# A graph layer and a ternary feed-forward block: weights transposed by DMA into a ring, and tiles in contiguous rows per group

## The reference

```python
# N=1250 nodes, E=20000 edges sorted by dst, D=512, FFN_DIM=1408, GROUP=128
msg_sum = segment_sum(x[src], dst);  deg = segment_sum(1, dst)
h = x @ W_self + (msg_sum / max(deg, 1)) @ W_neigh + b        # x here: layernorm(x)
h = where(h >= 0, h, 0.01 * h)
x = x + h / max(sqrt(sum(h * h)), 1e-12)

wg = w.reshape(o, i // 128, 128)                               # for w_gate, w_up, w_down
scale = mean(abs(wg)) + 1e-5
wq = clip(round(wg / scale), -1, 1) * scale                    # ternary times a scale
gate = xn @ wq_gate.T;  up = xn @ wq_up.T                      # xn = layernorm(x)
x = x + (silu(gate) * up) @ wq_down.T
```

## Time and profile before

| | before |
|---|---|
| time, median of 3 runs | 364.9 us (363.96 to 366.82) |
| the profiled execution: its own time | 365.24 us |
| the profiled execution: span | 363.3 us |
| mean granted TensorE clock | 0.987 |
| busy: TensorE, weight loads | 329.8 us (91%), 249.6 us (69%) |
| busy: VectorE, ScalarE, GpSimd | 304.6 us (84%), 238.0 us (66%), 163.1 us (45%) |
| chain that ended last, by engine | PE 58%, DVE 26%, ACT 10%, issue 3% |
| the same, line 1320 (the FFN matmuls) | 39% |
| line 1320, matmuls with x as moving operand | 528, 192.4 us busy |
| line 1320, matmuls with h as moving operand | 264, 94.8 us busy |
| line 1114, VectorE's takes of g, u and acc | 260, 167.9 us busy |

### The profile page before, as it was taken

One profiled execution on the slowest core, in us unless ns is written; L12 is line 12 of the kernel. 1 busy time (PEld: TensorE's weight loads), 2 busy tenths in 40 slices (PEclk: granted clock), 3 DMA queues, 4 the chain that ended last, 5 costly groups with the idle time before them and its releaser, 6 DMA issues.

```text
span 363.3 us, 5834 instructions
## 1 busy us (share of the span) xinstructions
PE 329.8 (91%) x1623; PEld 249.6 (69%) x1623; DVE 304.6 (84%) x789; ACT 238.0 (66%) x637; POOL 163.1 (45%) x223
## 2 busy tenths in 40 slices
PE   1997879899999999999687999999999999999992
PEld 0443335554545578777476898989899898889991
DVE  3569999899889248999696998999999989999994
ACT  2155958899787136774656768668777678676670
POOL 7000000110010590110003466888788787799992
PEclk9999999999999999999988999999999999999998
DMA  7961322233232001200000000000000000000215
GB/s 226 291 159 33 86 58 78 68 88 87 59 82 79 3 3 35 74 22 2 0 1 2 0 3 0 3 0 0 2 3 2 0 0 3 0 3 0 73 44 169
DMA packets 9412, 16.69 MB, mean 46 GB/s; under 512 B 1062, under 2 KB 1886, under 8 KB 9378
## 3 DMA queue, kind: packets, MB, share of 16 engines
q1 hardware_dynamic: 9300, 16.21, 15.9%
q10 hardware_dynamic: 78, 0.08, 0.1%
HBM read 13.73 MB, written 2.56 MB: 45 GB/s over the span
## 4 chain that ended last, share of the span: by engine, by line
PE 58%; DVE 26%; ACT 10%; issue 3%; POOL 1%; DVEq 0%; ACTq 0%; POOLq 0%
PE bank L1320 39%; PE bank L1208 7%; PE bank L1250 5%; DVE tq_gu L901 4%; DVE hot_dst L1005 3%; ACT mag_early L690 3%; DVE tq_d L901 2%; DVE hot_src L996 2%; ACT a_t L742 2%; DVE bn L1061 2%; ACT hot_src L675 2%; DVE x_sb L1058 2%; DVE z L1040 1%; PE bank L1232 1%; PE bank L1156 1%
## 5 line engine op out<-in xcount | busy, mean ns | idle before, releaser
L1320 PE MATMUL bank<-x_hi,t_gu 128*128 128x378 f32 (+1 forms) x264 | 96.9, 367 | 3.6 <-DVE x_lo L1075 2.8
L1320 PE MATMUL bank<-x_lo,t_gu 128*128 128x378 f32 (+1 forms) x264 | 95.5, 362 | 0.0
L1208 PE MATMUL bank<-w_sb,xnT 128*125 128x512 f32 x160 | 86.9, 632 | 4.8 <-ACT z L725 4.1
L1114 DVE SCALAR_TENSOR_TENSOR g_acc<-bank,nscale,g_acc 128x378 f32<-128x378 f32 (+1 forms) x99 | 64.3, 650 | 12.1 <-PE bank L1320 10.8
L612 POOL TENSOR_SCALAR thr<-absum 128x4 f32<-128x4 f32 (+1 forms) x34 | 10.7, 315 | 121.5 <-ACT mag_early L690 97.2
L1114 DVE SCALAR_TENSOR_TENSOR u_acc<-bank,nscale,u_acc 128x378 f32<-128x378 f32 (+1 forms) x99 | 64.1, 647 | 0.0
L633 POOL TENSOR_TENSOR acc<-acc,d_one 128x378 f32<-128x378 f32 (+1 forms) x58 | 60.9, 1052 | 0.1
L643 POOL TENSOR_TENSOR hh<-sg,u_acc 128x378 f32<-128x378 f32 (+1 forms) x32 | 35.1, 1098 | 57.4 <-ACT sg L830 57.3
L1320 PEld LDWEIGHTS bank<-x_hi,t_gu 128*128 128x128 f32 x264 | 51.1, 193 | 8.1 <-DVE x_lo L1075 3.5
L1320 PEld LDWEIGHTS bank<-x_lo,t_gu 128*128 128x128 f32 x264 | 51.0, 193 | 3.6
L1167 PEld LDWEIGHTS bank<-hot_dst,hot_src 128*125 128x125 bf16 x157 | 20.8, 137 | 42.0 <-DVE hot_dst L1005 23.0
(11 more groups left out here) (136 smaller groups left out, 558.5 us busy)
## 6 DMA issues: line engine op xcount, KB each, us to landing
raw<-in_L_ffn_w_gate SPq DMA_DIRECT2D x11, 256.0 KB, 2.7
raw<-in_L_ffn_w_up SPq DMA_DIRECT2D x11, 256.0 KB, 2.6
out_x<-x_sb SPq DMA_DIRECT2D x10, 224.0 KB
raw<-in_L_ffn_w_down SPq DMA_DIRECT2D x8, 256.0 KB, 2.7
x_sb<-in_x SPq DMA_DIRECT2D x1, 1344.0 KB
w_sb<-in_L_gnn_W_neigh SPq DMA_DIRECT2D x1, 1024.0 KB, 6.0
w_sb<-in_L_gnn_W_self SPq DMA_DIRECT2D x1, 1024.0 KB, 7.3
raw<-in_L_ffn_w_down SPq DMA_DIRECT2D x4, 192.0 KB, 2.3
```

What stands on the lines that cost most here:

```text
L1114: nc.vector.scalar_tensor_tensor(out=to, in0=bank_of(u, what)[:, 0:w], scalar=nscale[:, j:j + 1], in1=to, op0=ALU.mult, op1=ALU.add).then_ ...
L1208: last = nc.tensor.matmul(to[0:TP, :], xnT[:, t, k * TP:(k + 1) * TP], w_sb[:, k, half * D:(half + 1) * D], start=k == 0, stop=k == KD - 1)
L1320: last = nc.tensor.matmul(to, w, parts[h], start=h == 0, stop=h == 1)
```

## The change

**The weights.** SyncE, behind its last load and a wait for all ternary weights (`sp.wait_ge(ternary, JOBS)`), issues a DMA transpose for each 128x128 block: 8 per gate-and-up turn, 4 per down turn, 22 turns, 132 in all. They go into `turned_gu` (3 slots) and `turned_d` (2 slots), which lie where `raw` was. A turn waits until the Sign copy has emptied its slot. ScalarE's Sign copies stand where they stood, wait for the DMAs of their slot and read the ring. TensorE's 132 weight transposes, the identity `ident_b` and the use of bank 7 for weights are gone; `TERNARY` lists in which turn ScalarE takes which weights. Of `BANK7` only tiles 7, 8 and 9 are left (`XBANK7`).

**The layout.** A group of nodes was tiles of 126 columns each with gaps between them; now its tiles stand side by side with 125 columns, and one more at the end where the sum is odd: widths 376, 376 and 500 (`CN`). `x1_hi` and `x1_lo` are one tensor per group, in which the columns of a k are one run; `acc` follows. The copies of line 762 and 1075 write four rows of 125 or 126 with a stride. `x1_high` waits for all ternary weights from tile 6 on, not from tile 8 on.

```diff
+    CN = [(b - a) * TP + (b - a) % 2 for a, b in CT]
+    C0 = [sum(CN[:c]) for c in range(len(CT))]
...
+    TURN_GU, TURN_D = 3, 2
+    turned_gu = place("turned_gu", [P, TURN_GU, 2 * D], BF16, "raw")
+    turned_d = place("turned_d", [P, TURN_D, D], BF16, "raw", TURN_GU * 2 * D * 2)
...
-    x1_hi = place("x1_hi", [P, NT, KD, TQ], F32R, "w")
-    x1_lo = place("x1_lo", [P, NT, KD * P], F32R, "xz")
+    x1_hi = [place(f"x1_hi{c}", [P, KD, CN[c]], F32R, "w", C0[c] * KD * 4) for c in range(len(CT))]
+    x1_lo = [place(f"x1_lo{c}", [P, KD, CN[c]], F32R, "xz", C0[c] * KD * 4) for c in range(len(CT))]
...
+            sp.wait_ge(ternary, JOBS)
+            for f, down in turns:
+                if (f, down) in old_turn:
+                    sp.wait_ge(t_done, turn_T[old_turn[f, down]] + 1)
+                i = turn_slot[f, down]
+                if not down:
+                    for a in range(2):
+                        for k in range(KD):
+                            sp.dma_start(turned_gu[:, i, a * D + k * P:a * D + (k + 1) * P],
+                                         tq_gu[:, a * NF + f, k * P:(k + 1) * P], transpose=True).then_inc(gu_turned[i], 16)
+                else:
+                    for o in range(KD):
+                        sp.dma_start(turned_d[:, i, o * P:(o + 1) * P], tq_d[:, o, f * P:(f + 1) * P],
+                                     transpose=True).then_inc(d_turned[i], 16)
...
             def ternary_out(f, down):
 
-                act.wait_ge(t_ready, turn_T["T", f, down] + 1)
+                i, uses = turn_slot[f, down], turn_use[f, down] + 1
...
-                    nc.scalar.activation(t_gu[:, t_slot[f], :, :].rearrange("p a d -> p (a d)"), bf(7)[:, 0:2 * D],
+                    act.wait_ge(gu_turned[i], 16 * 2 * KD * uses)
+                    nc.scalar.activation(t_gu[:, t_slot[f], :, :].rearrange("p a d -> p (a d)"), turned_gu[:, i, :],
                                          ACT.Sign).then_inc(t_done, 1)
...
-                    to = bank_of(u, what)[:, 0:width(u)].rearrange("p (t s) -> p t s", s=TQ)
-                    parts = (x1_hi[:, a:b, k, :], x1_lo[:, a:b, k * TQ:(k + 1) * TQ])
+                    parts = (x1_hi[c][:, k, :], x1_lo[c][:, k, :])
...
-                if (u, what) in BANK7:
-                    through_bank7(BANK7[u, what])
+                if (u, what) in XBANK7:
+                    t = XBANK7[u, what]
+                    if t - 1 in XBANK7.values():
+                        pe.wait_ge(xlo_done, t)
+                    transpose_xn(t, normed1, bank[7], x1n_T, place_of(t)[2])
```

More of the change, by code:

```diff
@@ L72, in gnn_ffn, with place_of @@
     TQ = 126
+    GAP = 128
     CT = [(0, 3), (3, 6), (6, NT)]
+    CN = [(b - a) * TP + (b - a) % 2 for a, b in CT]
+    C0 = [sum(CN[:c]) for c in range(len(CT))]
+    NQ = sum(CN)
+    def place_of(t):
+        c = max(c for c in range(len(CT)) if CT[c][0] <= t)
+        a, b = CT[c]
+        rows = TP + (CN[c] - (b - a) * TP if t == b - 1 else 0)
+        return c, (t - a) * TP, rows
     CW = 512
@@ L398, in gnn_ffn @@
             took[p] = 1 + sum(by_act(*q) == by_act(*p) for q in pieces[:i])
-        BANK7 = {(0, "U3"): ("X", 7), (1, "U1"): ("T", 1, 0), (1, "U3"): ("X", 8), (2, "U1"): ("T", 0, 1), (2, "U3"): ("X", 9),
-                 (3, "U3"): ("T", 1, 1), (4, "U3"): ("T", 2, 0), (6, "U3"): ("T", 3, 0), (7, "U3"): ("T", 2, 1),
-                 (8, "U3"): ("T", 3, 1)}
+        TERNARY = {1: (1, 0), 2: (0, 1), 3: (1, 1), 4: (2, 0), 6: (3, 0), 7: (2, 1), 8: (3, 1)}
         for f in range(3, NF - 3):
-            BANK7[first_of[f], "U3"] = ("T", f + 1, 0)
+            TERNARY[first_of[f]] = (f + 1, 0)
             if f < NF - 4:
[L407 to L410, removed]
+                TERNARY[last_of[f]] = (f + 1, 1)
+        for v, what in ((NU - 11, (NF - 1, 0)), (NU - 10, (NF - 2, 0)), (NU - 9, (NF - 3, 1)),
+                        (NU - 8, (NF - 1, 1)), (NU - 7, (NF - 2, 1))):
+            TERNARY[v] = what
         t_slot = [f % 2 for f in range(NF - 1)] + [2]
-        through7 = [("T", 0, 0)] + [BANK7[e] for e in sorted(BANK7)]
-        turn_T = {e: i for i, e in enumerate(e for e in through7 if e[0] == "T")}
+        turns = [(0, 0)] + [TERNARY[v] for v in sorted(TERNARY)]
+        turn_T = {e: i for i, e in enumerate(turns)}
+        assert sorted(turns) == [(f, down) for f in range(NF) for down in range(2)]
+        turn_slot, turn_use = {}, {}
+        for down, slots in ((0, TURN_GU), (1, TURN_D)):
+            for i, e in enumerate(e for e in turns if e[1] == down):
+                turn_slot[e], turn_use[e] = i % slots, i // slots
+        old_turn = {e: old for e in turns for old in turns
+                    if old[1] == e[1] and turn_slot[old] == turn_slot[e] and turn_use[old] == turn_use[e] - 1}
+        XBANK7 = {(0, "U3"): 7, (1, "U3"): 8, (2, "U3"): 9}
+        gu_turned = [sem(f"gu_turned{i}") for i in range(TURN_GU)]
+        d_turned = [sem(f"d_turned{i}") for i in range(TURN_D)]
         piece_ready = sem("piece_ready")
@@ L1224, in _ @@
                     degree_columns(c).then_inc(deg_ready, 1)
-            def ternary_in(f, down):
-                pe.wait_ge(ternary, JOBS if down else JOBS1)
-                if not down:
-                    for a in range(2):
-                        for k in range(KD):
-                            last = nc.tensor.transpose(bf(7)[:, a * D + k * P:a * D + (k + 1) * P],
-                                                       tq_gu[:, a * NF + f, k * P:(k + 1) * P], ident_b[:])
-                else:
-                    for o in range(KD):
-                        last = nc.tensor.transpose(bf(7)[:, o * P:(o + 1) * P], tq_d[:, o, f * P:(f + 1) * P], ident_b[:])
-                last.then_inc(t_ready, 1)
             general_pe(pe, any_outside)
@@ L1294, in _ @@
                             pe.wait_ge(d_added, added[v, f"D{o}"])
+                    c, o, _ = place_of(u)
                     for k in range(KD):
-                        last = nc.tensor.transpose(bank_of(u, what)[0:TP, k * P:(k + 1) * P], acc[:, k, u * TQ:u * TQ + TP], ident[:])
+                        last = nc.tensor.transpose(bank_of(u, what)[0:TP, k * P:(k + 1) * P], acc[:, k, C0[c] + o:C0[c] + o + TP], ident[:])
                     last.then_inc(piece_ready, 1)
```

88 lines of the change are left out of this document (36 added, 52 removed).

## The result

| | before | after |
|---|---|---|
| time, median | 364.95 us (4 runs) | 380.75 us (4 runs, 379.63 to 382.42) |
| ratio | | 1.043, 95% interval 1.038 to 1.048 |
| span of the profiled execution | 363.3 us | 378.3 us |
| mean granted TensorE clock | 0.987 | 0.95 |
| busy: TensorE, VectorE, ScalarE, GpSimd | 329.8, 304.6, 238.0, 163.1 us | 330.5, 303.2, 237.7, 164.5 us |

The changed kernel is 4.3% slower. TensorE has 132 instructions less and is busy as long as before, since it ran for a part of the time at a lower clock (0.95 in the mean); and it waits more.

What follows compares the result with a forecast made beforehand. TensorE bounds the kernel before, SyncE's DMA transposes after: 166.3 + 170.3 + 2.3 = 338.9 us, then 40.2 less 0.7 plus 0.5 gives span 378.9; plus 1.9, about 381 us. Range 351 to 394 us.

Steps and rivals of the forecast that it cites:

- What bounds the kernel, and what takes its place: TensorE bounds at 14.70 us per block; then SyncE's DMA transposes set the pace from about 230 us, 15.6 us per block.
- The pace c: Time from one DMA transpose to the next in SyncE's queue, taken as 1.3 us; break-even at 1.18 us.
- the upper bound: Highest c considered: each DMA transpose lands before the next is issued, 2.3 us, the shortest landing.
- the lower bound: Lowest c considered: what a plain load of 128 rows takes in SyncE's queue, 0.328 us.
- the overlap: Rival: DMA transposes in SyncE's queue overlap, c up to 1.10 us, so weights arrive in time; 354 us, chance 0.38.
- The sum: Whole kernel: last four transposes land at 338.9 us, span 378.9 us, plus 1.9 us gives 380.8, say 381 us.
- The price on TensorE: Weight transposes on TensorE cost 0.305 us plus 0.525 us, so each block gives back 0.83 us.
- The layout: Matmuls on TensorE: x falls to h's step, 0.24 us, and narrower columns save 0.08 us; 0.32 us per block.
- The case on the other side: Rival that DMA transposes overlap and don't bound: 12.6 us less, 1.6 us back, 354 us; chance 0.38.
- The loss of 1.6 us that I had put down to VectorE: Added if transposes overlap: VectorE's block is as long as TensorE's, neither can always wait for the other; 1.6 us.
- The clock: After stops TensorE's matmuls run at the lower clock level, costing 1 to 2 us each time, mostly hidden in queue waits.

Runs made afterwards that it cites:

- experiments 3 and 4: Changed kernel with gate-and-up transposes resized: 3, two DMAs of 128x512 per turn, 353.57 us; 4, two DMAs of 64x128 per 128x128 block, 492.55 us (single run).
- experiment 7: Changed kernel with the old layout (126-column tiles with gaps) and two 128x512 transposing DMAs per gate-and-up turn: 355.98 us, ratio 0.974 to the kernel before.
- experiment 5: Changed kernel with only gate and up transposed by DMA (88 of 128x128), down back on TensorE and bank 7: 357.73 us, ratio 0.979 to the kernel before.

## Why the prediction was right

- **What bounds the kernel, and what takes its place.** Right. TensorE set the pace, and the row of DMA transposes took over. SyncE's queue shows no gap over 0.5 us from 164.62 to 336.48 us, and ScalarE waits with a DMA as releaser, in every turn of gate and up from 238.8 us on (put at about 230). Its copies of two blocks then lie 15.88 us apart (254.53 to 270.41), where I had 15.6.
- **The pace c.** I had chosen 1.3 us as the middle of 0.328 and 2.3 us; it is 1.275 us, 1.30 in the mean of the whole row, which has a few longer ones. That the middle hit so closely is partly luck: the upper bound, a DMA that lands before the next is issued, was not the mechanism (landing is 2.4 us), and the lower bound was a load from HBM, while a copy within SBUF holds the queue 0.60 us. The chance of 0.38 for the overlap was fair on what the rows before showed, but experiments 3 and 4 show that the price is one per DMA, which I had not separated from one per byte ("a transpose has to take a block apart by 2-byte elements"). That reason was wrong: the bytes cost nothing between 64x128 and 128x512.
- **The price beside a regular copy.** Two transposes follow each other at 1.275 us and land after 2.4 us; a plain copy of the same block holds the queue 0.60 us and lands after 1.8 us. The Trainium skill's 1309 ns for this path ("VectorE: DVE Perf Modes", section "The three transpose paths") agree with the distance of two transposes and not with the landing. Its rule that transposing DMAs are as fast as regular ones ("Advanced Engine Details and Errata", section "X-Bar Transpose (TRN2)") doesn't hold for blocks of this size here: 1.233 us to 0.60 us in the queue, 2.4 us to 1.8 us until they land.
- **The sum.** Start 164.6 (put at 166.3: the stages ahead ran 1.7 us earlier; in the other runs with a ring it was 164.8 to 165.9), last landing 335.2 + 2.4 = 337.6 us (338.9), span 378.3 (378.9), time 380.75 (381). One step was not as I had it: the turn that decides is not the last one, the down weights of block 9, but the gate-and-up weights of block 9, which are ready at 322.3 us. After them stand 56.0 us; behind the same copy before, at 306.7 us, stood 56.6 us. The last 12 transposes, of down, were in time. Both ways of counting come to the same within a microsecond, by the balance of the order: 12 transposes take 15.3 us, and the three turns between are about as long.
- **The price on TensorE.** Right in size: 0.82 us of a block in the old layout (experiment 7) for 0.83, and for gate and up alone 0.50 us (experiment 5) for 0.525. Layout alone to both with wide DMAs is 362.44 - 353.57 = 8.9 us; I had put 11 x 0.83 = 9.1 us.
- **The layout.** Right in its mechanism, since x and h matmuls have nearly the same step now, and mis-sized a little: 3.0 us for 3.5, 0.23 us per block for 0.32.
- **The case on the other side.** Its time was put at 354 us; with transposes that are not the bound it is 353.6 and 354.2 us (wide) and 353.8 us (plain copies). The loss of 1.6 us that I had put down to VectorE is of the right size, but not for that reason alone. A block takes 13.72 us, not 13.55: of the 0.17 us, 0.09 are the layout's mis-sizing, 0.01 the price on TensorE, and only some 0.07 are lost when both gains come together, with VectorE busy 39.41 of 40 us. That VectorE causes these 0.07 is argued, not shown.
- **The clock.** Right: the stop of 4.41 us is followed by the lower level up to 245.1 us. Eight steps of 0.41 us in place of 0.23 there (241.83 to 245.13 us) cost about 1.5 us, where I had 1 to 2, and it is hidden in the wait for the queue.

## What to carry to other kernels

Price a row of DMA transposes by their number, not their bytes: here 1.23 us in the issuing queue for each, from 64x128 to 128x512. So give each as many columns as the layout allows (512 were the most tried); the same change with 66 DMAs in place of 132 was 3% faster than before and not 4% slower. And look at who takes the result in a fixed order: 12 transposes took 15.3 us per block of 13.7 us of work, a queue some 10% too slow, and it stopped every engine behind ScalarE.

## What the runs showed of the hardware

- A DMA transpose holds SyncE's queue 1.229 us (64x128), 1.233 us (128x128), 1.267 us (128x512), and lands after 2.4 us in all three cases.
- A plain copy within SBUF of 128 rows of 256 bytes holds the queue 0.60 us and lands after 1.8 us; a load of 128 rows of 2 KB from HBM 0.33 us and 2.6 us.
- A few transposes hold the queue longer: 5 of the 132 of the changed kernel, 1.69 to 2.28 us. What causes this was not tried.
- 132 transposes in 172 us beside a busy TensorE didn't slow its matmuls: the step of 500 columns with x is 0.225 to 0.23 us beside them, and that of 504 columns was 0.23 us before without.
